# Conditioning a block in one round with two PSUM banks, and three banks instead of four for the up product

## The reference

```python
w = weights[conditions]                          # (128, 32, 32)
h = einsum('bct,bcd->bdt', x, w)                 # the conditioning
logits = h @ gate_w                              # 256 x 8
routing_weights, _ = top_k(logits, 2)
shared = square(relu(h @ up_w)) @ down_w         # 256 x 1024, 1024 x 256
moe = (h @ expert_weight) * routing_weights.sum(-1)
y = shared + moe
out = x + (y - mean(y)) * rsqrt(var(y) + 1e-5) * ln_gamma + ln_beta
```

## Time and profile before

| | |
|---|---|
| median of 3 runs | 234.11 us (234.08 to 234.24) |
| the profiled execution's own time | 233.91 us |
| its span | 232.2 us |
| PE busy (matmuls) | 223.0 us, 96% of the span |
| weight loads on PE | 190.3 us, 82% |
| DVE busy | 147.7 us, 64% |
| POOL busy | 132.4 us, 57% |
| ACT busy | 106.9 us, 46% |
| granted PE clock, mean | 0.998 of full speed |

### The profile page before, as it was taken

How to read it: one execution, slowest core, us unless ns; L and a number is a source line. 1 busy time by engine, 2 the same in 40 slices (tenths; PEclk the granted TensorE clock), 3 DMA queues, 4 the chain that set the end, 5 groups by cost and what they waited for, 6 DMA issues and landing times.

```text
span 232.2 us, 3940 instructions
## 1 busy us (share of the span) xinstructions
PE 223.0 (96%) x1240; PEld 190.3 (82%) x1240; DVE 147.7 (64%) x376; ACT 106.9 (46%) x185; POOL 132.4 (57%) x122
## 2 busy tenths in 40 slices
PE   7798989999999999999999999999999999999991
PEld 2577868888888888888888888888888888888991
DVE  1357886666655666666666766556666666666885
ACT  2468963454454444444444544454445344444100
POOL 5326974377546564566554675466644675466522
PEclk9999999999999999999999999999999999999999
DMA  5539132130503002000200002000110002000111
GB/s 186 130 116 299 32 96 61 48 97 10 184 10 97 9 11 83 1 0 0 93 0 0 3 1 92 0 3 0 42 48 3 0 0 92 3 0 1 49 67 68
DMA packets 17015, 11.81 MB, mean 51 GB/s; under 512 B 6753, under 2 KB 16482, under 8 KB 16994
## 3 DMA queue, kind: packets, MB, share of 16 engines
q1 hardware_dynamic: 16482, 11.50, 16.2%
q10 hardware_dynamic: 384, 0.03, 0.1%
q0 software_dynamic: 128, 0.02, 0.0%
HBM read 7.35 MB, written 4.19 MB: 50 GB/s over the span
## 4 chain that ended last, share of the span: by engine, by line
PE 89%; DVE 2%; SPq 2%; issue 2%; ACT 1%; DMA 1%; POOLq 0%; POOL 0%; DVEq 0%
PE up_ps L256 37%; PE down_ps L316 25%; PE down_ps L318 13%; PE hid_ps L224 6%; PE moe_ps L334 3%; PE moe_ps L332 3%; PE moe_ps L333 3%; SPq L172 1%; DMA wd<-in_L_cond_weights_dram 1%; DVE up_lo L481 1%; ACT relu L370 0%; ACT up_hi L376 0%; POOLq L39 0%; SPq L152 0%; POOL rstd L544 0%
## 5 line engine op out<-in xcount | busy, mean ns | idle before, releaser
L529 POOL TENSOR_TENSOR sq_lo<-square,sq_hi 128x512 fp32r<-128x512 f32 x64 | 83.6, 1309 | 64.4 <-DVE square L426 64.2
L316 PE MATMUL down_ps<-down_hl,sq_hi 128*128 128x512 f32 x248 | 88.8, 393 | 0.6 <-issue 0.6
L318 PE MATMUL down_ps<-down_hl,sq_lo 128*128 128x256 f32 x248 | 69.6, 280 | 0.0
L426 DVE SCALAR_TENSOR_TENSOR square<-up_ps,relu 128x512 f32<-128x512 f32 x64 | 43.9, 687 | 36.2 <-ACT relu L370 36.1
L316 PEld LDWEIGHTS down_ps<-down_hl,sq_hi 128*128 128x128 f32 x248 | 46.5, 188 | 11.5 <-ACT down_hl L382 1.0
L370 ACT ACTIVATE relu<-up_ps 128x512 f32<-128x512 f32 x64 | 38.2, 597 | 34.4 <-PE up_ps L256 34.2
L256 PE MATMUL up_ps<-hid_hi,up_hi 128*128 128x512 f32 x128 | 51.8, 405 | 0.3 <-ACT hid_hi L357 0.3
L256 PE MATMUL up_ps<-hid_hi,up_lo 128*128 128x512 f32 x128 | 50.3, 393 | 0.4 <-DVE up_lo L481 0.4
L318 PEld LDWEIGHTS down_ps<-down_hl,sq_lo 128*128 128x128 f32 x248 | 46.7, 188 | 2.3
L372 ACT ACTIVATE sq_hi<-relu 128x512 fp32r<-128x512 f32 x64 | 40.6, 634 | 2.0
L362 ACT ACTIVATE moe<-moe_ps,scale 128x256 f32<-128x256 f32 x32 | 15.2, 475 | 54.5 <-DVE scale L436 54.5
(11 more groups left out here) (44 smaller groups left out, 199.5 us busy)
## 6 DMA issues: line engine op xcount, KB each, us to landing
x_sb<-in_x_dram SPq DMA_DIRECT2D x8, 512.0 KB, 3.5
out_dram<-result SPq DMA_DIRECT2D x7, 512.0 KB, 2.9
wd<-in_L_cond_weights_dram SPq DMA_DIRECT2D x116, 4.0 KB, 1.6
result<-in_L_ffn_up_w_dram SPq DMA_DIRECT2D x2, 512.0 KB, 5.3
x_sb<-in_L_ffn_down_w_dram SPq DMA_DIRECT2D x1, 1024.0 KB, 5.3
out_dram<-result SPq DMA_DIRECT2D x4, 128.0 KB, 1.7
eg_raw<-L_ffn_expert_weight_dram SPq DMA_DIRECT2D x1, 256.0 KB, 2.5
wd<-in_L_cond_weights_dram ACTq DMA_DIRECT2D x8, 4.0 KB, 2.8
```

The lines of the kernel that those rows point to most:

```text
L316: pe.matmul(dst[:, :], a_hi, down_hl[:, c, :, :].rearrange("p s t -> p (s t)"), start=(c == 0), stop=False)
L318: mm = pe.matmul(dst[:, T:2 * T], a_lo, down_hl[:, c, 0, :], start=False, stop=(c == CH - 1))
L426: dve.scalar_tensor_tensor(square[:, c % 2, :], up_ps[c % UPB][:, :], 0.0, relu[:, c % 2, :], ALU.max, ALU.mult).then_inc(square_done, 1)
L529: pool.tensor_tensor(sq_lo[:, j % 2, c, :], square[:, c % 2, :], sq_hi[:, j % 2, c, :].bitcast(f32), ALU.subtract).then_inc(sq_lo_done, 1)
```

## The change

The conditioning of a block was done in two rounds in two slots: columns 0 to 127 in slot 4 (slot 2 from block 1 on), columns 128 to 255 in slot 6 (slot 4), both into the one bank `hid_ps`, apart from the very first block, whose second half used `moe_ps`. Now both halves are done one behind the other in the first of these slots, 16 PE instructions instead of twice 8, and each half has a bank of its own. ACT and DVE evacuate the first half in the slot behind the round, as before, and the second half in the slot after that, one slot earlier than before. The bank comes from `up_ps`, which keeps three. So that the banks are used in turn across blocks too, the bank of a chunk is now chosen by `(CH * j + c) % UPB`. PE's wait before an up chunk becomes one for the square of three chunks before, where it was four; this wait has UPB in it and its line is not edited.

```diff
-UPB = 4
+UPB = 3
-        hid_ps = bank("hid_ps")
+        hid_ps = [bank(f"hid_ps{k}") for k in range(K)]
-        def round_at(j):
-            return (4, 6) if j == 0 else (2, 4)
-        def round_bank(j, k):
-            return moe_ps if j == 0 and k == 1 else hid_ps
+        def conditioned_at(j):
+            return 4 if j == 0 else 2
...
-            def conditioning(j, k):
-                if k == 0:
-                    pe.wait_ge(x_landed[j], 16)
...
-                pe.wait_ge(hid_lo_done, K * j + k)
-                for t in range(TILES):
-                    mm = condition(j, k, t)
-                mm.then_inc(hid_done, 1)
+            def conditioning(j):
+                pe.wait_ge(x_landed[j], 16)
...
+                for k in range(K):
+
+                    pe.wait_ge(hid_lo_done, K * (j - 1) + k + 1)
+                    for t in range(TILES):
+                        mm = condition(j, k, t)
+                    mm.then_inc(hid_done, 1)
...
-                return pe.matmul(up_ps[c % UPB][:, :], ...
+                return pe.matmul(up_ps[(CH * j + c) % UPB][:, :], ...
...
-                    if j + 1 < BLOCKS and c in round_at(j):
-                        conditioning(j + 1, round_at(j).index(c))
+                    if j + 1 < BLOCKS and c == conditioned_at(j):
+                        conditioning(j + 1)
...
-                    if j + 1 < BLOCKS and c - 1 in round_at(j):
-                        hidden(j + 1, round_at(j).index(c - 1))
+                    if j + 1 < BLOCKS and c - 1 - conditioned_at(j) in range(K):
+                        hidden(j + 1, c - 1 - conditioned_at(j))
```

More of the change, by code:

```diff
@@ L223, in condition @@
                 g = TILES * j + t
-                return pe.matmul(round_bank(j, k)[:, P * t:P * t + P], x_sb[:, g, P * k:P * k + P], wd[:, g, :],
+                return pe.matmul(hid_ps[k][:, P * t:P * t + P], x_sb[:, g, P * k:P * k + P], wd[:, g, :],
                                  start=True, stop=True)
@@ L239, in conditioning_first @@
                 condition(0, 1, LOWER + 1).then_inc(hid_done, 1)
-            def conditioning(j, k):
-                if k == 0:
-                    pe.wait_ge(x_landed[j], 16)
[L244 to L248, removed]
-                pe.wait_ge(hid_lo_done, K * j + k)
-                for t in range(TILES):
-                    mm = condition(j, k, t)
-                mm.then_inc(hid_done, 1)
+            def conditioning(j):
+                pe.wait_ge(x_landed[j], 16)
+                if j == 1:
+                    pe.wait_ge(wd_second_landed[0], 16 * Q * (TILES - 1))
+                    pe.wait_ge(wd_second_landed[1], 16 * Q)
+                else:
+                    pe.wait_ge(wd_landed[j], 16 * Q * TILES)
+                for k in range(K):
[3 more added lines that the diff above has]
+                    mm.then_inc(hid_done, 1)
             def up_product(j, c, w, k, h, n):
-                return pe.matmul(up_ps[c % UPB][:, :], w[:, k, P * c:P * c + P], h[:, j % 2, k, :], start=(n == 0),
+                return pe.matmul(up_ps[(CH * j + c) % UPB][:, :], w[:, k, P * c:P * c + P], h[:, j % 2, k, :], start=(n == 0),
                                  stop=(n == 3 * K - 1))
@@ L356, in hidden @@
                 act.wait_ge(hid_done, K * j + k + 1)
-                act.activation(hid_hi[:, j % 2, k, :], round_bank(j, k)[:, :], ACT.Copy).then_inc(hid_hi_done, 1)
+                act.activation(hid_hi[:, j % 2, k, :], hid_ps[k][:, :], ACT.Copy).then_inc(hid_hi_done, 1)
             def scale_moe(j, t):
@@ L369, in rectify @@
                 wait(act, square_done, n - 1)
-                act.activation(relu[:, c % 2, :], up_ps[c % UPB][:, :], ACT.Relu).then_inc(relu_done, 1)
+                act.activation(relu[:, c % 2, :], up_ps[(CH * j + c) % UPB][:, :], ACT.Relu).then_inc(relu_done, 1)
                 act.wait_ge(relu_done, n + 1)
@@ L417, in hidden @@
                 dve.wait_ge(hid_hi_done, K * j + k + 1)
-                dve.tensor_tensor(hid_lo[:, j % 2, k, :], round_bank(j, k)[:, :],
+                dve.tensor_tensor(hid_lo[:, j % 2, k, :], hid_ps[k][:, :],
                                   hid_hi[:, j % 2, k, :].bitcast(f32), ALU.subtract).then_inc(hid_lo_done, 1)
@@ L425, in square_up @@
                 wait(dve, sq_lo_done, n - 1)
-                dve.scalar_tensor_tensor(square[:, c % 2, :], up_ps[c % UPB][:, :], 0.0, relu[:, c % 2, :],
+                dve.scalar_tensor_tensor(square[:, c % 2, :], up_ps[(CH * j + c) % UPB][:, :], 0.0, relu[:, c % 2, :],
                                          ALU.max, ALU.mult).then_inc(square_done, 1)
```

## The result

The changed kernel took 234.70 us (median of 13 runs, 234.49 to 234.90), the kernel before 234.06 (13 runs): a ratio of 1.0027, interval 1.0019 to 1.0035, that is 0.64 us slower. The direction was forecast, and the range held it, but the case taken as the likeliest (A, 236.1) did not happen. The loss has the shape of case B, and is 0.2 smaller than B's 0.84.

The account below looks back on a forecast made before the run. PE, with matmuls filling 96% of the span, was taken to bound the kernel. 233.91 + 1.88 (block 0's engine order) + 0.12 (rounds) = 235.91, banks 0, with 0.20 added for the median 236.1; range 234.0 to 236.6, chance 0.82.

Parts of the forecast that it names:

- case A: Block 0's down-weight split: POOL's `sq_lo` 6 starts before DVE's part 1; second half tile +1.88, 236.1 us, chance 0.42.
- case B: Block 0's down-weight split: DVE's part 1 starts before POOL's `sq_lo` 6; second half tile +0.72, 235.0 us, chance 0.28.
- Banks: PE's up chunks with three banks: no wait on a square or conditioning bank, cost 0.
- the 3.5 us forecast: Margin at PE's up chunks: square done 3.0 us after chunk start, three slots at least 6.5 in block 0.
- The round: Merged conditioning on PE: 16 cost twice 0.89; +0.02 a block, +0.12 over blocks 1 to 6, block 0 zero.
- the four lengths of the sum: PE's steady slots after the change: 4.55, 3.51, 2.77 and 3.53, together 14.36 for 14.34 before.
- The order in slots (0,5) to (1,1): ACT, DVE and POOL at block 0's end: later `relu` 5 delays the down-weight split; +1.88 taken, bounds -1.4 to +3.0.
- the exclusion of DVE's split and POOL: A `split_down` on DVE and a POOL operation exclude each other; the later ends 0.55 (DVE) or 1.15 (POOL) behind.
- The wait on `hidden`: PE's 0.4 wait at the weight load disappears, but nothing reaches the end while part 3 is late.
- C: Block 0's split: DVE and POOL don't collide in the new alignment; 234.1 us, no change, chance 0.14.
- D: Faster: both block 0 down-weight waits gone, 232.8 us, or merging saves a fixed round price, 233.6; together chance 0.06.
- E: Another turn lost, or an evacuation late in steady blocks: above 236.6 us, chance 0.10.

Follow-up runs that it names:

- the banks alone: Kernel before with three up banks and two conditioning banks, rounds and evacuations in their old slots: 234.01 us, ratio 1.000.
- the later blocks alone: Kernel before with the new banks, merged round and earlier evacuation only from block 1 on: 234.11 us, ratio 1.0003.
- The forcing run: Changed kernel plus a small DVE memset ahead of part 1 of the down-weight split, so POOL's `sq_lo` 6 starts first: 236.01 us, ratio 1.0083.
- that program: Changed kernel with block 0's second-half `hidden` evacuated in slot 7 again, one slot later: 235.19 us, ratio 1.0048.

## Why the prediction was right or wrong

**Banks: right.** No wait on a square, and 234.01 with the banks alone. The margin was thinner than the 3.5 us forecast: in these slots 2.4 (the square of chunk 6 ends at 28.43, chunk 9 starts at 30.83), and 1.1 in the start-up, which the forecast didn't look at.

**The round: right.** A round of 16 takes 1.78, twice 0.89. The steady slots have the four lengths of the sum. The time of the later blocks alone, +0.08 with an interval of 0.2 to either side, is too coarse to measure the 0.14; that number is the trace's, over five blocks. The forecast had 0.12 for six.

**The order in slots (0,5) to (1,1): the right mechanism, the wrong turn.** This is the step that failed: the term of case A, +1.88 at the second half tile, was taken, and +0.57 measured, near case B's +0.72. The later `relu` 5, the exclusion of DVE's split and POOL, the first half tile, and case A itself (236.1 forecast, 236.01 when forced) came out as worked. Which case happens did not, and the range held the result only because it held B as well. The sentence that failed is "POOL asks for `sq_lo` 6 at 28.61. DVE asks for part 1 at 28.58 + 0.03 = 28.61. A tie, within my 0.01." On the chip, counted from `relu` 5, POOL asked at 28.51 - 23.98 = 4.53, as forecast (28.61 - 24.09 = 4.52), but DVE at 28.35 - 23.98 = 4.37, 0.15 earlier, and with that DVE won the turn.

The error is in two distances of ACT. "`scale_moe` ... `hidden` ... +0.43" and "`relu` 6 +0.59" were read from 24.89 to 25.32 and from 27.01 to 27.60. At the second place of each pair stands a `relu` that needs a finished up chunk. Chunk 5, whose `relu` surely waited for PE, had its first matmul at 21.53 and its `relu` at 23.20, 1.67 later. Chunk 7's first matmul in the kernel before, in PE's timeline:

```profile
25.93 0.48 PE L256 MATMUL up_ps<-hid_hi,up_hi 128*128 128x512 f32 x1
...
26.94 0.62 PE L256 MATMUL up_ps<-hid_lo,up_hi 128*128 128x512 f32 x2
```

and 25.93 + 1.67 = 27.60 is the `relu` to the hundredth: PE set it, not ACT. (The last two matmuls of chunk 7, in the row at 26.94, end at 27.56, and `relu` 7 starts 0.04 behind that. For chunks 5 and 6 the same distance is 0.04 too.) Chunk 6 stands behind an expert tile, not behind a round, so its first matmul is the 0.08 shorter that the prediction names:

```profile
23.73 0.39 PE L256 MATMUL up_ps<-hid_hi,up_hi 128*128 128x512 f32 x1
```

23.73 + 1.67 - 0.08 = 25.32, again the `relu`. In the changed kernel ACT is late and doesn't wait there, and the distances are 0.37 and 0.48. Together they are 0.06 + 0.11 = 0.17 less, and DVE's lead at the turn was 0.16. POOL's `sq_lo` 6 had nothing to gain from it, since it waits for square 6, and that stood behind part 0 on DVE. The first distance could have been read from the kernel before, where `scale_moe` at 30.35 is followed by a `relu` whose chunk had long been done, 0.38 later:

```profile
30.73 0.59 ACT L370 ACTIVATE relu<-up_ps 128x512 f32<-128x512 f32 x1
```

The second could not: wherever in the kernel before a `relu` stands right behind a `hidden`, it waits for PE. With 0.38 for the first alone, DVE would have asked 0.05 ahead of POOL, and the forecast would have been B.

With the true distances case B comes out: part 3 on ACT 0.17 earlier, at B's 31.81 - 0.17 = 31.64 (31.53 measured, with everything 0.11 earlier from `relu` 5 on), and part 3 on DVE held by `sq_lo` 7. What is left of B's 0.72 is 0.57, because part 1 was done 0.15 earlier, and the POOL operations behind it, up to `sq_lo` 7, moved forward by that.

The error was small against the numbers it was made of and large in what it decided. The forcing run shows the price: 236.01 against 234.70.

**The wait on `hidden`: right.** It went, and its 0.4 didn't reach the end: the first half tile starts 0.23 earlier behind the round, and the wait on part 3 is longer by that.

**Rivals.** C, no collision in the new alignment, did not happen: part 3 took 1.51. D and E did not happen.

## What to carry to other kernels

A distance between two starts on an engine is that engine's own pace only if the second instruction waited for nothing. The profile may show no idle time before an instruction that was released in the very moment when the engine became free: check when its input was ready before using the distance elsewhere. Where two engines exclude each other and a forecast ends in a tie, both sides are likely results, and a range with both is the honest answer. In a kernel whose one engine is full, look for loss in the one-time work that runs beside it; here waits that keep POOL out of DVE's way for four instructions, with two `add_beta` moved, were worth 0.4% on the kernel before, more than the change cost. A delay ahead of such a shared turn need not show as a delay behind it: here it showed as another turn lost.

## What the runs showed of the hardware

How strongly two starts of DVE and POOL decide: DVE ahead by 0.16, it takes 0.68 and POOL 1.69; POOL ahead by 0.14, it takes 1.30 and DVE 1.70. In the changed kernel too the one that comes second ends 0.54 (DVE, parts 0 and 3) or 1.16 to 1.17 (POOL, `sq_lo` 6 and `add_beta`) behind the other's end. In between, with both starts at 27.98, POOL was undisturbed in the one execution profiled. Not expected was the spread of that program's six times, one of 234.38 and five of 235.15 to 235.38.
